# Gather of neighbours by one-hot tiles: a batch's sixteen tiles divided among GpSimd (4), VectorE (8) and ScalarE (4)

## The chip, the cores and the metric

The kernel runs on one core of one Trainium2 chip. The metric is the device time of one execution in microseconds (us); the lower the better. TensorE is called PE here, VectorE DVE, ScalarE ACT, GpSimd POOL, and SyncE SP, as in the profile.

## The reference

One layer of a network: a cross attention over a point cloud, then a state-space mixer, then a small feed-forward block. Only the first part matters here. It has 16 batches of 512 points with 32 features. Four space-filling curves (`M = 4` methods) give four orders of the points, and each point's neighbours are the 10 points of a window in each order:

```python
def _window_inds(sorted_idx, k=K):
    start = jnp.maximum(0, i - k // 2)
    end = jnp.minimum(N, i + k // 2 + 1)
    pos = jnp.minimum(start[:, None] + jnp.arange(k)[None, :], (end - 1)[:, None])
    return jnp.take(sorted_idx, pos, axis=1)
...
neigh = gather(feats, inds)
gf = jnp.concatenate([jnp.broadcast_to(center, (B, N, k, C)), neigh - center], axis=-1)
```

What is gathered goes into a small attention over each window, a linear map, a normalisation and a maximum. This is done for two layers, the second on the features that the first gives.

## The kernel before

The program runs in stages, with a barrier between each and the next: `keys_and_ranks` (the rank of each point in each order), then for each of the two layers `gather_windows` and `window_attention`, with `instance_norm` between the layers, then `join_features`, `mamba_prepare`, `mamba_mix` and `feed_forward`. The change touches `gather_windows` alone, which runs twice.

`gather_windows` puts the features of a batch into the order of each curve by matmul with one-hot matrices. For a batch there are 16 one-hot tiles, 4 methods by 4 tiles of 128 points: a tile is 128 points by `EXT` = 576 places (f16), with a one where the point's rank equals the place. There are two ways to make a tile:

- DVE compares `place` with the rank in one instruction (line 695).
- ACT takes the absolute value of the distance in one activation (`apart`, line 763, three buffers), then relu(1 - distance) in a second one (line 776).

Before the change DVE makes tiles 0 to 9 (`HOT = 10`) and ACT tiles 10 to 15 (`LATE = 6`). POOL only clears parts of `cen`, `cen16` and `QT` at the start (lines 665 to 669). ACT starts when these are cleared.

A batch passes through these steps. The order on each engine is that of its `step` function, which `steps` unrolls by four batches; `at(1)` is the batch before the one of `at(0)`.

- SP loads the batch's features `fb` (32 channels by 512 points), stores the centre copies `cen16`, and stores `QT` to DRAM in four transfers of 360 KB.
- PE turns `fb` so that points lie on partitions (`ptok`) and spreads it over the four methods (`pcen`). Then, for the batch before, it gathers: 64 matmuls of 288 columns with the one-hot tiles and the high and low halves `t16` and `l16` into `pext`, and raises `gathered`. It starts these when all tiles of that batch are there.
- ACT copies `t16`, makes its first two tiles, copies `pext` of the batch before into `ext` (line 795), makes the rest of its tiles and copies `pcen` into `cen` and `cen16` (lines 804, 805).
- DVE makes `l16` (line 688; for the first batch line 693, in the middle of its tiles), its tiles, and then for the batch before the subtraction of the centres from the windows: three of 1710 columns into `QT` (line 707) and a small one (line 712).

The tiles have two buffers, by the batch's parity. `gathered` begins at 2 and counts gathers: whoever writes tiles of batch b waits for `gathered >= b + 1`, the end of the gather of batch b - 2. `ext`, `cen` and `QT` have four buffers.

Other lines that the prediction speaks of: in the window attention POOL subtracts a maximum (`Dm`, line 1069) while DVE reduces (lines 1029, 1033). In the mixer DVE splits a weight (`Wo`, line 2025) and POOL adds squares (`sqsum`, lines 2078, 2082). In the feed-forward block DVE splits `u` (line 2285) while POOL adds to `uf` (line 2313).

Of the kernel before, what the change touches and what calls it, by code (L numbers as in the profile page):

```python
# [10 lines left out]
ALU = mybir.AluOpType  # L11
ACT = mybir.ActivationFunctionType
X = mybir.AxisListType.X

B, S, D = 16, 32, 512
N = D
C = S
NT = N // 128
M = 4
# [526 lines left out]
def steps(eng, step, T, U):  # L546


    for s in list(range(U)):
        step(s % U, lambda lag, s=s: (s - lag, (s - lag) // U) if 0 <= s - lag < T else None)  # L550
    with eng.Fori(1, T // U) as i:
        for k in range(U):
            step(k, lambda lag, k=k: (i * U + (k - lag), i + (k - lag) // U))
    for s in range(T, T + U):
        step(s % U, lambda lag, s=s: (s - lag, (s - lag) // U) if 0 <= s - lag < T else None)


def gather_windows(nc, io, scratch, layer, O, feats, runs, perm, rank, fixed):


    with ExitStack() as ctx:
        def sb(name, shape, dt=F32):
            return ctx.enter_context(nc.sbuf_tensor(name + layer, shape, dt))
# [3 lines left out]
        def sem(name):  # L567
            used.append(ctx.enter_context(nc.semaphore(name + "_gw" + layer)))
            return used[-1]

        H2 = EXT // 2
        ident, rep, place = (fixed[name] for name in ("ident", "rep", "place"))
# [3 lines left out]
        onehot = sb("onehot", [128, 2, M * NT, EXT], F16)  # L576
        apart = sb("apart", [128, 3, EXT], F16)
# [17 lines left out]
        rank_turned = sem("rank_turned")  # L595
        apart_ready = sem("apart_ready")
        late_hot = sem("late_hot")
        gathered = sem("gathered")
        ext_ready = sem("ext_ready")
        cen_ready = sem("cen_ready")  # L600
        q_v = sem("q_v")
        q_out = [sem(f"q_out{k}") for k in range(4)]
        QV = PTS + 1
        HOT = 10
        LATE = M * NT - HOT
        SL = 128 // O
        QO = 16 * (M + 2)
        ZEROS = 6
# [8 lines left out]
        def first(b):  # L617

            return isinstance(b, int) and b == 0

        def late(b):

            return isinstance(b, int) and b >= B - 2
# [38 lines left out]
        @block.gpsimd  # L662
        def _(pool):
            for tile in (cen, cen16):
                nc.gpsimd.memset(tile[:, :, LEAD:LEAD + 1], 0.0).then_inc(zeroed, 1)
                nc.gpsimd.memset(tile[:, :, N + 1:PADN], 0.0).then_inc(zeroed, 1)
            turns = QT[:, :, :, :].rearrange("p k g x -> p k (g x)").rearrange("p k (w x) -> p k w x", x=32 * RES)
            nc.gpsimd.memset(turns[:, :, :, PTS * K * RES:], 0.0).then_inc(zeroed, 1)
            nc.gpsimd.memset(turns[:, :, NSUB // RES:, 0:PTS * K * RES], 0.0).then_inc(zeroed, 1)
            pool.wait_ge(zeroed, ZEROS)  # L670
            for k in range(4):
                pool.sem_inc(q_out[k], QO)

        @block.vector
        def _(dve):
# [6 lines left out]
            def step(k, at):  # L682
                if at(0):
                    (b, _), h = at(0), k % 2
                    dve.wait_ge(gathered, b + 1)
                    if not first(b):
                        dve.wait_ge(t16_ready, b + 1)
                        v.tensor_tensor(l16[:, h, :], ptok[:, h, 0:NT * C], t16[:, h, :],
                                        ALU.subtract).then_inc(l16_ready, 1)
                    for mt in range(HOT):  # L690
                        if first(b) and mt == HOT // 2:
                            dve.wait_ge(t16_ready, b + 1)
# [25 lines left out]
        @block.tensor  # L718
        def _(pe):
            pe.sem_inc(f_used, 2)  # L720
            pe.sem_inc(gathered, 2)

            def step(k, at):
                if at(0):
                    (b, i), h = at(0), k % 2
                    pe.wait_ge(f_in[h], (i * 32 + 16 * (k // 2 + 1)) * len(runs))
                    pe.wait_ge(l16_ready, b + 1)
                    pe.wait_ge(cen_ready, b + 1)
                    for t in range(NT):
                        last = nc.tensor.matmul(ptok[:, h, t * C:(t + 1) * C], fb[:, h, t * 128:(t + 1) * 128],  # L730
                                                ident[:, :], start=True, stop=True)
                    last.then_inc(tokens_out, 1)
                    nc.tensor.matmul(pcen[:, h, 0:N], rep[:, :], fb[:, h, :], start=True, stop=True).then_inc(f_used, 1)
                if at(1):
                    (b, _), k = at(1), (k - 1) % 4
                    h = k % 2
                    pe.wait_ge(l16_ready, b + 3)
                    pe.wait_ge(hot_ready, b * HOT + HOT)
                    pe.wait_ge(late_hot, b * LATE + LATE)
                    pe.wait_ge(ext_ready, b + 1)  # L740
                    for e in range(2):
                        for n in range(2 * NT):
                            half, t = (t16, l16)[n // NT], n % NT
                            for m in range(M):
                                last = nc.tensor.matmul(pext[m * C:(m + 1) * C, h, e, 0:H2],
                                                        half[:, h, t * C:(t + 1) * C],
                                                        onehot[:, h, m * NT + t, e * H2:(e + 1) * H2],
                                                        start=n == 0, stop=n == 2 * NT - 1)
                    last.then_inc(gathered, 1)

            steps(pe, step, B, 4)

        @block.scalar
        def _(act):
            act.sem_inc(cen_ready, 2)
            act.sem_inc(ext_ready, 2)
            act.wait_ge(zeroed, ZEROS)
            act.wait_ge(rank_turned, 2)

            def distance(b, j):  # L760

                mt = HOT + j
                nc.scalar.activation(apart[:, j % 3, :], place[:, :], ACT.Abs,
                                     bias=minus_rank[:, bass.ds(b + perm[mt // NT] * B, 1), mt % NT])\
                    .then_inc(apart_ready, 1)

            def hots(b, h, j0, j1):

                if j0 == 0:
                    distance(b, 0)  # L770
                for j in range(j0, j1):
                    if j + 1 < LATE:
                        act.wait_ge(late_hot, b * LATE + max(j - 1, 0))
                        distance(b, j + 1)
                    act.wait_ge(apart_ready, b * LATE + (j + 1))
                    nc.scalar.activation(onehot[:, h, HOT + j, :], apart[:, j % 3, :], ACT.Relu, scale=-1.0,
                                         bias=unit[:, :]).then_inc(late_hot, 1)

            def step(k, at):
                if at(0):  # L780
                    (b, i), h = at(0), k % 2
                    if first(b):
                        act.wait_ge(gathered, b + 1)
                        hots(b, h, 0, 2)
                    act.wait_ge(tokens_out, b + 1)
                    act.wait_ge(gathered, b + 1)
                    nc.scalar.activation(t16[:, h, :], ptok[:, h, 0:NT * C], ACT.Copy).then_inc(t16_ready, 1)
                    if not first(b):
                        act.wait_ge(late_hot, b * LATE)
                        hots(b, h, 0, 2)  # L790
                if at(1):
                    (b, _), k1 = at(1), (k - 1) % 4
                    act.wait_ge(gathered, b + 3)
                    act.wait_ge(q_v, b * QV + QV)
                    nc.scalar.activation(ext[:, k1, :].rearrange("p (e x) -> p e x", e=2), pext[:, k1 % 2, :, 0:H2],  # L795
                                         ACT.Copy).then_inc(ext_ready, 1)
                if at(0):
                    (b, i), h = at(0), k % 2
                    hots(b, h, 2, LATE)
                    act.wait_ge(f_used, b + 3)  # L800
                    act.wait_ge(q_out[k], i * QO + QO)
                    act.wait_ge(q_v, b * QV + QV)
                    for s0, n0, n1 in RUNS:
                        nc.scalar.activation(cen16[:, k, s0:s0 + n1 - n0], pcen[:, h, n0:n1], ACT.Copy)
                        last = nc.scalar.activation(cen[:, k, s0:s0 + n1 - n0], pcen[:, h, n0:n1], ACT.Copy)
                    last.then_inc(cen_ready, 1)
                if at(3) and late(at(3)[0]):
                    (b, r), k3 = at(3), (k - 3) % 4
                    act.wait_ge(q_v, b * QV + 5 * QV)
                    for m in range(M // 2, M):  # L810
                        store_windows(act, k3, r, m)

            steps(act, step, B, 4)
# [1683 lines left out]
```

## Time and profile before

| | us |
|---|---|
| median of 3 runs | 2252.63 (2251.91 to 2253.1) |
| the profiled execution | 2251.6 |
| its span | 2249.8 |
| busy PE, DVE, ACT, POOL | 1857.1, 1865.7, 1620.7, 1007.2 |

The profile is of one execution; the span runs from its first to its last recorded instruction. A timeline row has its start, its duration, engine, line of the program, what it writes and reads with the shapes, how many instructions were merged into it (x5) and, in brackets, how long the engine had been idle and who ended the wait. A row that merges several instructions lasts from the first's start to the last's end.

### The profile page before, as it was taken

To read this page: it belongs to the slowest core of one execution; us is meant where nothing else is said; L and a number is where in the kernel's file an instruction comes from. 1 tells how busy PE (TensorE), PEld (TensorE's weight loads), DVE (VectorE), ACT (ScalarE), POOL (GpSimd) and SP (SyncE) were. 2 spreads that over 40 slices of the span, in tenths; PEclk is the share of its full clock that TensorE was granted. 3 is DMA by queue.
4 is the path that set the end of the run, shared out by engine and by line. 5 is a ranking of instruction groups with operands and counts; after the bars stand their busy time and mean duration, and the time that the engine had idled before them with its cause. 6 is when DMAs were issued, how large, how long until landed. Compare 5 with 4: busy or idle time off the path is not lost. (4 is left out here: it accounts for less than half of the span.)

```text
span 2249.8 us, 100270 instructions
## 1 busy us (share of the span) xinstructions
PE 1857.1 (83%) x37656; PEld 1296.1 (58%) x37656; DVE 1865.7 (83%) x3775; ACT 1620.7 (72%) x3324; POOL 1007.2 (45%) x995
## 2 busy tenths in 40 slices
PE   3866648888886665699999997687999999999957
PEld 1333347777775433599999996333544454454422
DVE  8879969999997798688888887865888888888874
ACT  5889948888886998699999996465455455555432
POOL 0000048999995000578888884002433444344412
PEclk9996679999998666899999998899999999999988
DMA  1127666555563477645555551203222222222210
GB/s 36 30 65 169 163 146 126 119 125 122 120 125 72 94 171 164 133 101 107 107 107 107 107 107 38 95 10 96 85 80 84 75 84 81 82 84 75 65 55 19
DMA packets 434892, 215.50 MB, mean 96 GB/s; under 512 B 301195, under 2 KB 404267, under 8 KB 434680
## 3 DMA queue, kind: packets, MB, share of 16 engines
q1 hardware_dynamic: 430272, 210.76, 39.8%
q10 hardware_dynamic: 4536, 3.66, 0.6%
q8 instruction: 48, 0.79, 0.2%
q14 instruction: 36, 0.29, 0.0%
HBM read 161.35 MB, written 52.86 MB: 95 GB/s over the span
## 5 line engine op out<-in xcount | busy, mean ns | idle before, releaser
L973 PE MATMUL pQ<-QM,QX 128*128 128x64 f16 (+1 forms) x5760 | 532.4, 217 | 1.6 <-issue 1.6
L971 PE MATMUL pQ<-neigh_lo,QX 128*128 128x32 f16 (+1 forms) x5760 | 520.9, 189 | 2.8 <-issue 2.8
L971 PEld LDWEIGHTS pQ<-neigh_lo,QX 128*128 128x128 f16 x5760 | 496.0, 103 | 5.2 <-issue 2.5
L973 PEld LDWEIGHTS pQ<-QM,QX 128*128 128x128 f16 x5760 | 487.8, 104 | 2.5 <-issue 2.3
L1069 POOL TENSOR_TENSOR Dm<-Sc,mx 128x450 f32<-128x450 f32 x384 | 365.9, 953 | 80.6 <-DVE mx L1029 80.6
L1076 POOL TENSOR_TENSOR Ap<-E,R 128x450 f32<-128x450 f32 x384 | 365.8, 953 | 68.0 <-DVE R L1042 57.8
L1106 ACT ACTIVATE Vs<-pQ 128x480 f32<-128x480 f32 (+1 forms) x384 | 295.7, 770 | 5.7 <-PE pH L999 4.1
L1038 DVE STREAM_TRANSPOSE AT<-Ap 128x480 f32<-128x480 f32 x384 | 259.2, 675 | 33.3 <-PE pH L999 10.9
L2067 POOL TENSOR_TENSOR MT<-cb,decay 128x512 f32 (+1 forms) x128 | 163.9, 1302 | 244.2 <-PEq L1835 147.4
L1119 ACT ACTIVATE E<-Dm 128x450 f32<-128x450 f32 x384 | 224.3, 584 | 60.5 <-POOL Dm L1069 60.4
L1029 DVE TENSOR_REDUCE mx<-Sc 128x15 f32<-128x450 f32 x384 | 223.8, 583 | 16.5 <-ACT Sc L1100 16.5
L1033 DVE TENSOR_REDUCE Z<-E 128x15 f32<-128x450 f32 x384 | 233.5, 608 | 0.0
L1100 ACT ACTIVATE Sc<-pQ 128x450 f32<-128x450 f32 x384 | 209.2, 545 | 14.7 <-PE pQ L973 14.6
L999 PE MATMUL pH<-AT,Vs 128*32 128x30 f32 x17280 | 177.2, 197 | 47.5 <-DVE AT L1038 41.9
L999 PEld LDWEIGHTS pH<-AT,Vs 128*32 128x32 f32 x17280 | 172.5, 110 | 67.8 <-DVE AT L1038 42.0
L707 DVE TENSOR_TENSOR QT<-ext,cen 128x1710 f16<-128x1710 f32 x96 | 180.6, 1936 | 28.5 <-ACT ext L795 23.9
L966 PE MATMUL pQ<-maskR,maskL 128*128 128x160 f16 (+1 forms) x960 | 143.1, 247 | 67.5 <-DMA QX<-scratch_q 40.5
L2082 POOL TENSOR_TENSOR sqsum<-sqsum,sq 128x512 f32<-128x512 f32 x56 | 85.0, 1518 | 245.4 <-ACT sq L1928 245.4
L1860 PE MATMUL pO<-Wo,yw 128*128 128x512 f16 x768 | 176.3, 379 | 13.9 <-DVE Wo L2025 13.9
L1842 PE MATMUL pG<-h,W 128*128 128x512 f16 x768 | 178.2, 382 | 9.3 <-DVE W L2049 8.4
L2035 DVE SCALAR_TENSOR_TENSOR cv_m<-pX,taps_m,cv_m 128x496 f32<-128x496 f32 (+2 forms) x192 | 137.6, 717 | 51.7 <-ACT cv_m L1937 33.5
L1942 ACT ACTIVATE hid<-cv_m 128x512 f32<-128x512 f32 x64 | 40.3, 630 | 189.5 <-DVE cv_m L2035 189.5
(382 smaller groups left out, 3743.3 us busy)
## 6 DMA issues: line engine op xcount, KB each, us to landing
QM<-scratch_q SPq DMA_DIRECT2D x192, 240.0 KB, 2.7
QX<-scratch_q SPq DMA_DIRECT2D x768, 60.0 KB, 2.4
scratch_q<-QT SPq DMA_DIRECT2D x120, 360.0 KB, 4.8
Wg<-in_in_proj SPq DMA_DIRECT2D x64, 256.0 KB, 2.7
Wh<-in_in_proj SPq DMA_DIRECT2D x64, 256.0 KB, 2.8
Wo<-in_out_proj SPq DMA_DIRECT2D x64, 256.0 KB, 2.7
W_s<-in_in_proj SPq DMA_DIRECT2D x16, 256.0 KB, 2.7
CT<-scratch_c SPq DMA_DIRECT2D x192, 11.2 KB, 2.2
```

The lines of the kernel that those rows point to most:

```text
L707: v.tensor_tensor(flat[:, 0:W3, n * K:(n + 1) * K, :], rows(ext, k, LEAD * K + HALF - 1 + n, (PTS * RES, W3), (1, K), (PTS, RES)), rows(ce ...
L971: nc.tensor.matmul(pQ[:, p, u // PB, o + 32:o + BW], qx[u], W["neigh_lo"][:, 0:O], start=False, stop=True, skip_group_check=True)
L973: last = nc.tensor.matmul(pQ[:, p, u // PB, o:o + BW], qx[u], qm[u], start=False, stop=True, skip_group_check=True)
L999: last = nc.tensor.matmul(pH[at0:at0 + 32, p, 32 * u:32 * u + PTS * K], Vs[:, first + slot, u * O + 32 * half:u * O + 32 * half + 32], AT[ ...
L1029: v.tensor_reduce(mx[:, p, :], valid(Sc[:, p, :]), X, ALU.max).then_inc(max_ready, 1)
L1033: v.tensor_reduce(Z[:, p, :], valid(E[:, p, :]), X, ALU.add).then_inc(summed, 1)
L1038: v.transpose(AT[:, k5 % NA, :], A[:, k5 % ND, :]).then_inc(turned, 1)
L1069: nc.gpsimd.tensor_tensor(valid(Dm[:, p, :]), valid(Sc[:, p, :]), mx[:, p, :].unsqueeze(2).to_broadcast([128, SUBS, PTS * K]), ALU.subtrac ...
L1076: nc.gpsimd.tensor_tensor(valid(A[:, p, :]), valid(E[:, p, :]), R[:, p, :].unsqueeze(2).to_broadcast([128, SUBS, PTS * K]), ALU.mult).then ...
L1100: nc.scalar.activation(like(Sc[:, (k - 1) % ND, :], 32, PTS * K), blocks(p, 0, PTS * K), ACT.Copy)\
L1106: nc.scalar.activation(like(Vs[:, kv % RV, :], O, O), blocks(p, 32, O), ACT.Copy).then_inc(vs_ready, 1)
L1119: nc.scalar.activation(valid(E[:, p, :]), valid(Dm[:, p, :]), ACT.Exp, scale=32.0 ** -0.5).then_inc(exped, 1)
```

## The change

POOL takes four tiles (`ASIDE = 4`), DVE keeps eight (`HOT = 8`), ACT keeps four (`LATE = 4`). The tiles in order are 0 to 7 by DVE, 8 to 11 by POOL, 12 to 15 by ACT. POOL's comparison is the same instruction as DVE's, with the same waits on `gathered`. Its loop over the batches is written out: 64 instructions per stage after the clearing. PE waits for POOL's tiles also, by a new semaphore.

```diff
+        aside_hot = sem("aside_hot")
...
-        HOT = 10
-        LATE = M * NT - HOT
+        HOT = 8
+        ASIDE = 4
+        LATE = M * NT - HOT - ASIDE
...
             for k in range(4):
                 pool.sem_inc(q_out[k], QO)
+            for b in range(B):
+                pool.wait_ge(gathered, b + 1)
+                for mt in range(HOT, HOT + ASIDE):
+                    at = b + perm[mt // NT] * B
+                    nc.gpsimd.tensor_scalar(onehot[:, b % 2, mt, :], place[:, :], rank[:, at, mt % NT:mt % NT + 1], None,
+                                            ALU.is_equal).then_inc(aside_hot, 1)
...
                     pe.wait_ge(late_hot, b * LATE + LATE)
+                    pe.wait_ge(aside_hot, b * ASIDE + ASIDE)
...
-                mt = HOT + j
+                mt = HOT + ASIDE + j
...
-                    nc.scalar.activation(onehot[:, h, HOT + j, :], apart[:, j % 3, :], ACT.Relu, scale=-1.0,
+                    nc.scalar.activation(onehot[:, h, HOT + ASIDE + j, :], apart[:, j % 3, :], ACT.Relu, scale=-1.0,
```

## Rows read from the trace of the kernel before

**Rows 1.** Groups by line and shape: busy us, mean ns, idle before.

```profile
L776 ACT ACTIVATE onehot<-apart,unit_g 128x576 f16<-128x576 f16 x192 | 165.7, 903 | 0.0
...
L695 DVE TENSOR_SCALAR onehot<-place,rank 128x576 f16<-128x576 f16 x320 | 96.1, 378 | 0.0
```

**Rows 2.** Timeline of DVE (start us, duration us), the two stages' ends.

```profile
126.39 3.42 DVE L695 TENSOR_SCALAR onehot<-place,rank 128x576 f16<-128x576 f16 x5
...
294.39 0.23 DVE L712 TENSOR_TENSOR QT<-ext,cen 128x60 f16<-128x60 f32 x1
...
734.14 3.42 DVE L695 TENSOR_SCALAR onehot<-place,rank 128x576 f16<-128x576 f16 x5
...
902.16 0.23 DVE L712 TENSOR_TENSOR QT<-ext,cen 128x60 f16<-128x60 f32 x1
```

**Rows 3.** Stretches: us; PE, PEld, DVE, ACT, POOL busy; PEclk, DMA, GB/s.

```profile
200.00:248.75 48.75, 32.19 (x371) 19.66 (x371) 44.45 (x76) 48.75 (x91) 0.00 (x0) 0.61 0.72 169
```

**Rows 4.** Timeline of ACT, two activations in a row.

```profile
210.48 0.91 ACT L763 ACTIVATE apart<-place,minus_rank 128x576 f16<-128x576 f16 x1
211.15 0.92 ACT L776 ACTIVATE onehot<-apart,unit_g 128x576 f16<-128x576 f16 x1
```

**Rows 5.** Timeline of DVE, one batch.

```profile
210.87 5.64 DVE L707 TENSOR_TENSOR QT<-ext,cen 128x1710 f16<-128x1710 f32 x3 [0.50 <-ACT ext L795]
...
216.85 0.29 DVE L688 TENSOR_TENSOR l<-ptok,t 128x128 f16<-128x128 f32 x1
217.06 2.88 DVE L695 TENSOR_SCALAR onehot<-place,rank 128x576 f16<-128x576 f16 x10
```

**Rows 6.** Timeline of PE from one gather to the next.

```profile
147.39 1.15 PE L745 MATMUL pext<-onehot,t 128*32 128x288 f16 x16 [2.01 <-ACT onehot L776]
...
151.35 1.91 PE L730 MATMUL ptok<-ident_g,fb 32*128 32x32 f32 x8
153.08 2.05 PE L733 MATMUL pcen<-fb,rep 32*128 32x512 f32 x2
157.14 1.15 PE L745 MATMUL pext<-onehot,t 128*32 128x288 f16 x16 [2.01 <-ACT onehot L776]
```

**Rows 7.** DVE lines (ns min/median/max), and timelines of POOL and DVE.

```profile
L2025 DVE SCALAR_TENSOR_TENSOR Wo<-Wo x64: 676/1755/1765, 1561.8 to 2158.3; 128x512 f16<-128x512 f32 x64
...
1804.08 1.44 POOL L2082 TENSOR_TENSOR sqsum<-sqsum,sq 128x512 f32<-128x512 f32 x1 [7.54 <-ACT sq L1928]
...
1804.31 1.76 DVE L2025 SCALAR_TENSOR_TENSOR Wo<-Wo 128x512 f16<-128x512 f32 x1
...
L2285 DVE TENSOR_TENSOR u_f<-u_f x9: 1195/1199/1203, 2197.5 to 2227.8; 115x512 f16<-115x512 f32 x9
L2285 DVE TENSOR_TENSOR u_f<-uf_f,u_f x3: 692/693/693, 2195.6 to 2220.1; 115x512 f16<-115x512 f32 x3
```

**Rows 8.** Timelines of ACT, DVE and PE, start of the first stage.

```profile
129.13 1.44 ACT L763 ACTIVATE apart<-place,minus_rank 128x576 f16<-128x576 f16 x2 [10.29 <-POOL QT L669]
...
132.97 1.48 DVE L695 TENSOR_SCALAR onehot<-place,rank 128x576 f16<-128x576 f16 x5
...
137.63 1.15 PE L745 MATMUL pext<-onehot,t 128*32 128x288 f16 x16 [1.99 <-ACT onehot L776]
...
142.56 1.94 DVE L707 TENSOR_TENSOR QT<-ext,cen 128x1710 f16<-128x1710 f32 x1 [0.76 <-issue]
```

**Rows 9.** A line of POOL (ns min/median/max).

```profile
L1069 POOL TENSOR_TENSOR Dm<-Sc,mx x384: 941/952/962, 311.2 to 1375.1; 128x450 f32<-128x450 f32 x192
```

**Rows 10.** Groups of POOL by line and shape.

```profile
L2078 POOL TENSOR_TENSOR sqsum<-sq,zero_m 128x512 f32<-128x512 f32 x8 | 8.4, 1045 | 31.8 <-ACT sq L1928 31.8
...
L2313 POOL TENSOR_TENSOR uf_f<-uf_f,u_f 115x512 f32<-115x512 f32 x9 | 11.4, 1266 | 57.5 <-DVE u_f L2280 57.5
...
L1058 POOL MEMSET QX<- 128x1920 f32 x4 | 6.7, 1700 | 0.0
...
L1056 POOL MEMSET QX<- 128x960 f32 x2 | 1.8, 902 | 0.0
```

## Prediction

> **What bounds the kernel now.** I read the list of costliest instruction groups first, because it says where the edited lines run and how much time they hold. The gather's lines are a small part of the program: the sixteen tiles of a batch are 320 comparisons on DVE and 192 pairs of activations on ACT [rows 1], over 16 batches in each of two gather stages. DVE's first and last instructions of the stages lie at 126.4 and 294.6 us and at 734.1 and 902.4 us [rows 2], so some 336 of the 2249.8 us can be touched.
>
> Second, the table of stretches, for five batches in the steady part of the first stage. ACT is busy 48.75 of 48.75 us, DVE 44.5, PE 32 at a granted clock of 0.61, POOL not at all, and the DMA engines 0.72 of the time [rows 3]. ACT sets the pace, but DVE is at 91%: it is the next limit, only 9% away.
>
> Third, the timeline of one batch, which turns shares into a period: PE begins a gather at 147.39 and the next at 157.14 us [rows 6], 9.75 us apart. An activation on 576 columns starts 0.67 us after the one before it, although each is recorded as lasting 0.9 us [rows 4]: durations on ACT overlap, so spacing is the price. Twelve of them are 12 x 0.665 = 8.0 us, and the remaining 1.75 us are ext, the centre copies and t16. DVE's batch is 5.98 us from the first subtraction into QT to the l16 subtraction, 0.21 us for that, 10 tiles spaced (2.88 - 0.37) / 9 = 0.279 us apart (0.37 being one alone), and the rest of the 9.75 us, 0.7, is waiting for ACT [rows 5]. PE's batch, where it doesn't wait, is 3.96 us of matmuls into pext (147.39 to 151.35) and 3.78 us for ptok and pcen (to 155.13), 7.7 us in all [rows 6].
>
> **ACT's part.** Two of six pairs go, so 4 x 0.665 = 2.66 us per batch: ACT's own need falls from 9.75 to 7.1 us.
>
> **DVE's part, alone.** Two of ten tiles go, 0.56 us: 5.98 + 0.21 + 8 x 0.279 = 8.42 us per batch. DVE would set the period even if POOL's tiles cost it nothing, since PE needs 7.7 us and ACT 7.1. DMA work per batch is 0.72 x 9.75 = 7.0 us, below all of these.
>
> **POOL's part.** It adds 64 comparisons per stage, read from place (SBUF) and written to onehot. POOL waits for nothing but `gathered`, so those of batch b start when the gather of b-2 has ended; DVE's tiles for b-1 lie ahead of the same point, and POOL has more than a period for four instructions. POOL issues no DMA here and nothing but the next tiles is queued behind its wait. PE's additional wait costs nothing, by that slack. So the cost isn't POOL's time. It is what POOL's instructions do to DVE's.
>
> The trace shows that. At 1804.3 us DVE's subtraction into Wo (both inputs in SBUF) takes 1.76 us while POOL's sum, begun at 1804.08, runs; its shortest is 0.68 and its median 1.76. POOL's sum takes 1.44 us there, 1.26 where it is alone, and at the end of the program the subtraction into u_f takes 1.20 us beside POOL's sum and 0.69 without it [rows 7, 10]. So two such instructions exclude each other, and back to back they take turns. The comparison into onehot shows it too: the first five of the stage take 3.42 us while POOL clears QT (ACT is released by the last clearing at 129.13), the next five 1.48 [rows 2, 8]. Against that, POOL's 384 subtractions Dm stay within 941 and 962 ns although DVE's reductions, with one SBUF input, fill that stage [rows 9]: those don't collide. The subtraction into QT (ext and cen, both in SBUF) is of the Wo kind, and the tiles are of the other colliding kind. That is 5.9 + 2.2 of DVE's 8.42 us. DVE will have no idle time in which POOL could slip in, so each of POOL's four instructions delays DVE once per batch.
>
> **The price of one collision.** Wo loses 1.76 - 0.68 = 1.08 us to a POOL instruction that takes 1.26 us when it is not held up [rows 7, 10]: the price c is POOL's duration p less 0.18 us. No row shows a comparison on POOL. From below: a clearing of 960 and 1920 f32 columns takes 902 and 1700 ns, 0.83 ns a column, so 576 columns that are only written would take 0.58 us; c = 0.40. From above: two full inputs, 512 columns in 1.26 us, so 576 in 1.42; c = 1.24. With one of its two inputs a repeated column it was 1045 ns for 512, so 1.17 for 576 [rows 10]. One input read and one output written lies between 0.58 and 1.17; I take p = 0.9, c = 0.72.
>
> The Trainium skill (GPSIMD Engine Reference, Elementwise — side-by-side cycle accounting) gives about 1.8 cycles of 1.2 GHz per element for a tight loop; an estimate from that page is 0.86 us for 576, which would make the total 2280. The trace has no row for it. The skill's page SBUF — State Buffer, section Who interferes with whom, says that the shared port pair is held for the full instruction and that the loser fully blocks. By that rule c would be all of 0.9 us and the total 2304; the Wo row has 0.18 us less, and I go by the row.
>
> **The start of a stage.** POOL's clearings end at 129.1 us as before [rows 8]. ACT then has 8 activations instead of 12 before the first gather, which started at 137.6 us [rows 8]: 2.7 us earlier at best. But POOL goes on to batch 1 at once, in the middle of DVE's second group of tiles for batch 0, and collides up to three times (2 us). I put the first subtraction into QT, which started at 142.56 us, at 140.5.
>
> **The sum.** From there to the end DVE does 14 times 8.42 us and the last two QT groups (5.98 + 5.91): 129.8 us; and 56 of the 64 collisions fall into it (batches 2 to 15): 56 x 0.72 = 40.3 us. The stage's last DVE instruction then ends at 140.5 + 129.8 + 40.3 = 310.6 us where it ended at 294.6 [rows 2]; the same arithmetic for before, 142.56 + 15 x 9.75 + 5.9, gives 294.7. So +16.0 us per stage. The second stage took as long, 168.2 us [rows 2], so +32 us. The period would be 8.42 + 2.88 = 11.3 us. The profiled execution took 2251.6 us, 1.0 below the median; 2251.6 + 32 = 2283.6, with that 1.0 some 2284 us. Bounds: c = 0.40 gives 292.7 us for the stage's end, -4 us in total, 2248; c = 1.24 gives 339.7, +90, 2342. The change breaks even at c = 0.43 (p = 0.61), close to the lower bound.
>
> **Rivals.**
> *No collisions.* POOL's single SBUF input doesn't get in the way of DVE. DVE's 8.42 us set the period; the first QT starts at 139.8; the end is 139.8 + 129.8 = 269.6, 25 us earlier per stage: 2202 us. For it: all POOL rows beside which a DVE instruction runs long have two inputs or none. Against it: the clearing has none and delayed the tiles.
> *Only the tiles collide, the QT subtractions don't.* This is the mechanism that ends on the other side at a middling price: the gather ends 3.9 us after the tiles, 2.1 us of QT work are left, and of POOL's 3.6 us about 1.5 reach into the tiles, two collisions, 1.4 us a batch. The period is 9.8 us, yet start and tail gain: 139.8 + 129.8 + 14 x 1.4 = 289.2, 5.4 us earlier per stage, 2241 us. It decides if QT stays at 1.94 us with a POOL instruction beside it. Against it: the rows of Wo and u_f, which are of QT's kind [rows 7].
> *POOL's comparison is slower than the two-input rows*, say 2 us for f16 and a comparison: c = 1.82, 56 x 1.82 = 102 us, 2406 us. Nothing in the trace speaks for it but the missing row.
>
> **How the numbers follow.** 0.76 for the forecast (own range 2248 to 2342), 0.09 for no collisions, 0.08 for tiles only, 0.07 for the slow comparison. A difference of 0.2% (4.5 us) is about what a measurement of this kernel can tell from no change. Of the forecast's 0.76 some 0.06 lie within that, near its lower bound, and 0.01 below. Faster is 0.09 + 0.08 + 0.01 = 0.18, same 0.06, slower 0.69 + 0.07 = 0.76. The range runs from just under the tiles-only case to the upper bound: 2238 to 2340.
>
> **What would show it.** In the changed profile: QT subtractions with POOL beside them at 1.94 + 0.7 = 2.6 us, some tiles at 1.1 us instead of 0.37; ACT waiting for `gathered` before ext; a period of 11.3 us; the stage's last subtraction at about 310 us; POOL comparisons near 0.9 us alone and longer by the DVE instruction they wait for. QT all at 1.94 us, or a period under 9.7, would prove me wrong; POOL comparisons at 0.6 us would leave the mechanism and take away the loss.

## The result, and the profile after

| | before | after |
|---|---|---|
| median, us | 2252.86 (2251.91 to 2253.12, 4 runs) | 2285.41 (2282.41 to 2289.04, 4 runs) |
| ratio, 95% interval | | 1.0135 (1.0117 to 1.0154) |
| span of the profiled execution, us | 2249.8 | 2283.5 |

The change makes the kernel 1.35% slower, 33 us, where 32 us were forecast. The first thing to see is the ends of the two stages. Timeline of DVE in the changed kernel, the rows that answer to [rows 2] and, for the first subtraction into QT, to [rows 8]:

```profile
141.64 1.94 DVE L715 TENSOR_TENSOR QT<-ext,cen 128x1710 f16<-128x1710 f32 x1 [0.66 <-issue]
...
311.75 0.23 DVE L720 TENSOR_TENSOR QT<-ext,cen 128x60 f16<-128x60 f32 x1
...
935.16 0.23 DVE L720 TENSOR_TENSOR QT<-ext,cen 128x60 f16<-128x60 f32 x1
```

The first stage ends at 311.98 us, 17.4 later than before (294.62). The second, whose first tile now starts at 750.26, takes 185.1 us where it took 168.2. So the whole loss lies in the two gather stages: 17.4 + 16.9 = 34.3 us, where the span grew by 33.7. The table of stretches for 200 to 290 us, before and after (columns as in [rows 3]):

```profile
200.00:290.00 90.00, 56.18 (x656) 34.26 (x656) 79.01 (x127) 85.37 (x158) 0.00 (x0) 0.59 0.72 167
```

```profile
200.00:290.00 90.00, 56.40 (x608) 36.54 (x612) 89.70 (x104) 59.02 (x115) 90.00 (x34) 0.58 0.60 141
```

ACT is relieved (59 us instead of 85). DVE is busy 89.7 of 90 us with fewer instructions, and POOL is busy all the time. TensorE's granted clock is nearly the same, 0.59 and 0.58. Whose instructions became longer stands in the list of groups, after (the tiles were 378 ns in [rows 1]):

```profile
L679 POOL TENSOR_SCALAR onehot<-place,rank 128x576 f16<-128x576 f16 x128 | 340.4, 2678 | 1.0 <-POOL QT L671 1.0
L715 DVE TENSOR_TENSOR QT<-ext,cen 128x1710 f16<-128x1710 f32 x96 | 193.1, 2063 | 1.2 <-issue 1.0
L703 DVE TENSOR_SCALAR onehot<-place,rank 128x576 f16<-128x576 f16 x256 | 148.0, 646 | 0.0
```

DVE makes 256 tiles instead of 320 and needs 148 us for them instead of 96. One batch shows how; DVE's timeline, one instruction a row, and POOL's under it:

```profile
284.18 0.28 DVE L696 TENSOR_TENSOR l<-ptok,t 128x128 f16<-128x128 f32 x1
284.38 0.35 DVE L703 TENSOR_SCALAR onehot<-place,rank 128x576 f16<-128x576 f16 x1
284.66 0.76 DVE L703 TENSOR_SCALAR onehot<-place,rank 128x576 f16<-128x576 f16 x1
285.34 0.84 DVE L703 TENSOR_SCALAR onehot<-place,rank 128x576 f16<-128x576 f16 x1
286.10 0.36 DVE L703 TENSOR_SCALAR onehot<-place,rank 128x576 f16<-128x576 f16 x1
...
288.12 0.78 DVE L703 TENSOR_SCALAR onehot<-place,rank 128x576 f16<-128x576 f16 x1
288.82 1.92 DVE L715 TENSOR_TENSOR QT<-ext,cen 128x1710 f16<-128x1710 f32 x1
290.67 2.40 DVE L715 TENSOR_TENSOR QT<-ext,cen 128x1710 f16<-128x1710 f32 x1
292.98 1.93 DVE L715 TENSOR_TENSOR QT<-ext,cen 128x1710 f16<-128x1710 f32 x1
294.95 0.57 DVE L720 TENSOR_TENSOR QT<-ext,cen 128x60 f16<-128x60 f32 x1
295.43 0.28 DVE L696 TENSOR_TENSOR l<-ptok,t 128x128 f16<-128x128 f32 x1
```

```profile
285.24 1.76 POOL L679 TENSOR_SCALAR onehot<-place,rank 128x576 f16<-128x576 f16 x1
286.98 1.76 POOL L679 TENSOR_SCALAR onehot<-place,rank 128x576 f16<-128x576 f16 x1
288.72 3.53 POOL L679 TENSOR_SCALAR onehot<-place,rank 128x576 f16<-128x576 f16 x1
292.23 4.27 POOL L679 TENSOR_SCALAR onehot<-place,rank 128x576 f16<-128x576 f16 x1
```

The period is 11.25 us (284.18 to 295.43); forecast was 11.3. But its parts are not those of the prediction. While POOL runs, two of three tiles of DVE start 0.68 to 0.76 us after the one before them instead of 0.28. Five such delays of 0.40 to 0.48 us, the last of them ahead of the first QT, stretch the eight tiles from 2.2 to 4.4 us. The three long subtractions into QT last 6.09 us in place of the 5.64 of [rows 5], by one of 2.40, and the small one 0.57 instead of 0.23 [rows 2]. That makes seven lengthened instructions of DVE in a batch, by 0.34 to 0.48 us each, for four tiles of POOL. POOL's tile lasts 1.76 us beside DVE's tiles and 3.5 to 4.3 us beside QT.

### The profile page after: what moved, and what is told of

The parts are those of the page before. It is cut to its first block and busy times, and to the rows that moved or that the text cites. A ratio compares the mean times of both kernels' runs of the same rounds, so it can differ in the third digit from the quotient of the medians.

```text
span 2283.5 us, 100046 instructions
## 1 busy us (share of the span) xinstructions
PE 1855.5 (81%) x37656; PEld 1302.3 (57%) x37656; DVE 1936.5 (85%) x3711; ACT 1538.6 (67%) x3196; POOL 1348.1 (59%) x1123
## 5 line engine op out<-in xcount | busy, mean ns | idle before, releaser
L679 POOL TENSOR_SCALAR onehot<-place,rank 128x576 f16<-128x576 f16 x128 | 340.4, 2678 | 1.0 <-POOL QT L671 1.0
L715 DVE TENSOR_TENSOR QT<-ext,cen 128x1710 f16<-128x1710 f32 x96 | 193.1, 2063 | 1.2 <-issue 1.0
L754 PE MATMUL pext<-onehot,t 128*32 128x288 f16 x1024 | 74.9, 442 | 133.4 <-POOL onehot L679 61.6
```

The source lines that it names most:

```text
L679: nc.gpsimd.tensor_scalar(onehot[:, b % 2, mt, :], place[:, :], rank[:, at, mt % NT:mt % NT + 1], None, ALU.is_equal).then_inc(aside_hot, 1)
```

## The experiments

The rival theory that this trace suggests is that POOL sets the pace itself: it never stands still, four of its tiles take a whole period, and PE's waits name it (8 waits, 30.5 us in the first stage, against 27.8 for DVE's tiles). I call the theory of the prediction A (DVE is lengthened, and DVE sets the time) and this one B.

### Four comparisons on POOL that nobody needs

```diff
 # the kernel before, 10 DVE, 6 ACT
+            for b in range(B):
+                pool.wait_ge(gathered, b + 1)
+                pool.wait_ge(spared, max(b * 4 - 4, 0))
+                for mt in range(8, 12):
+                    nc.gpsimd.tensor_scalar(spare[...], place[:, :], rank[...], None, ALU.is_equal).then_inc(spared, 1)
```

> The kernel before (tiles 10 DVE, 0 POOL, 6 ACT), and POOL makes four comparisons per batch into a spare buffer that nobody reads or waits for. Theory A (POOL's instructions lengthen DVE's, and DVE sets the time): DVE's own 8.98 us per batch plus the 2.83 us that the changed kernel's trace shows for four of POOL's tiles (11.25 - 8.42) is 11.8 us; the period goes from 9.75 to 11.8, 14 or 15 periods in two stages: +60 us, 2312 us. Theory B (POOL's own pace, 11.25 us for four tiles, holds back PE, and DVE's longer instructions are hidden): nobody waits for POOL here, so 2253 us, unchanged.

Measured: 2310.34 us, ratio 1.0243 (1.0217 to 1.0268). Nobody waits for POOL, PE's tiles all come from DVE and ACT, and still 57 us are lost. Nor is POOL at its own limit here: from the seventh batch on it stands idle for 3.5 to 3.8 us before each batch, waiting for the gather (75.2 us in 20 waits). B is refuted; A's 2312 was right. From DVE's timeline of this run, the tiles of one batch:

```profile
223.60 5.57 DVE L704 TENSOR_SCALAR onehot<-place,rank 128x576 f16<-128x576 f16 x10
```

Ten tiles last 5.57 us, where they last 2.88 in [rows 5]. The three subtractions into QT that follow last 5.63 us, as ever: in this run only 3 of the 48 of each stage are longer. The cost lands nearly whole on the tiles and on the small subtraction.

### Three tiles on POOL

```diff
-        ASIDE = 4
+        ASIDE = 3
```

> The changed kernel with POOL's fourth tile given to ACT (8 DVE, 3 POOL, 5 ACT). Theory A: DVE's 8.42 us plus 3 x 0.71 us = 10.55 us per batch; the stage's last DVE instruction at 141.6 + 14 x 10.55 + 11.9 = 301 us against 294.7 before: +13 us, 2266 us. Theory B: POOL's pace falls to 3 x 2.81 = 8.4 us, so the period is about 8.5 us and the total 2208 us, faster than before.

Measured: 2273.78 us, 1.0083 (1.0062 to 1.0104), far from B's 2208, and 8 us above A's 2266. DVE's timeline has the batch's small subtraction at these places:

```profile
224.45 0.65 DVE L720 TENSOR_TENSOR QT<-ext,cen 128x60 f16<-128x60 f32 x1
...
225.22 4.51 DVE L703 TENSOR_SCALAR onehot<-place,rank 128x576 f16<-128x576 f16 x8
...
235.31 0.65 DVE L720 TENSOR_TENSOR QT<-ext,cen 128x60 f16<-128x60 f32 x1
```

The period is 10.86 us, only 0.4 less than with four tiles: the eight tiles are still 4.5 us long, since two of the three POOL tiles fall beside them and the third reaches into them. Against the 8.24 us that DVE needs alone for eight tiles (shown below) that is 0.87 us for a POOL tile, not the 0.71 that I had carried over.

### POOL clears instead of comparing

```diff
 # against the run with four comparisons that nobody needs
-                    nc.gpsimd.tensor_scalar(spare[...], place[:, :], rank[...], None, ALU.is_equal).then_inc(spared, 1)
+                    nc.gpsimd.memset(spare[...], 0.0).then_inc(spared, 1)
```

> As the run with four spare comparisons, but POOL clears the spare buffer four times per batch (writes 576 columns, reads nothing). Theory A in the form of the prediction (any POOL instruction costs DVE its duration less 0.18 us): four clearings of about 0.6 us cost 1.7 us, period 10.7 us, +26 us, 2279 us. Theory A in a narrower form (a POOL instruction that only writes collides with DVE's tile comparisons but not with the subtraction into QT): the clearings start when a gather ends, which is when DVE does QT, and are over before its tiles: 2253 us. Theory B: 2253 us.

Measured: 2253.16 us, 0.9993 (0.9982 to 1.0003): nothing lost. POOL's line and DVE's line for QT in this run (ns min/median/max):

```profile
L679 POOL MEMSET spare<- x128: 573/573/1466, 129.3 to 877.7; 128x576 f16 x128
...
L714 DVE TENSOR_TENSOR QT<-ext,cen x96: 1932/1935/1942, 142.3 to 900.1; 128x1710 f16<-128x1710 f32 x96
```

Three of the four clearings of a batch run beside a QT subtraction, at 0.57 us, without either being longer. The first begins during DVE's last tiles and waits for them (1.08 to 1.47 us in the batches at 209.6, 218.8 and 228.8 us), and it costs them nothing. The prediction's price, the length of the POOL instruction less 0.18 us, is wrong for a clearing at these places.

### What POOL's comparison takes alone

```diff
 # the kernel before; ahead of POOL's clearings, 24 instructions, each waiting for the last
+            for n in range(24):
+                pool.wait_ge(widened, n)
+                form[n // 3]().then_inc(widened, 1)
```

> The kernel before, and at the start of each gather stage, ahead of POOL's clearings, 24 instructions on POOL alone, each waiting for the last, three of each form: clear 576 f32; comparison 576 f16 as in the change; multiplication instead of comparison; comparison of 288 columns; comparison f32 to f32; comparison with a constant instead of the rank; product of two f16 tiles; clear 576 f16. DVE stands still for most of it. What sets the 1.74 us of POOL's tile? If it is DVE's contention, the comparison takes the predicted 0.9 us here. If it is POOL's own speed, 1.72 us. If the comparison is slow and not the f16 or the column count, the multiplication takes about 0.9 to 1.2 us; if it is the f16, the f32 form does. The 288 columns take half, 0.9 us, if it goes by columns. The kernel is longer by the 24 instructions twice, some 50 to 60 us.

Measured once: 2316.68 us, 63 more than before (50 to 60 were expected). The groups of POOL in this run:

```profile
L670 POOL TENSOR_SCALAR spare<-place,rank 128x576 f16<-128x576 f16 x6 | 10.6, 1767 | 0.6
L671 POOL TENSOR_SCALAR spare<-place,rank 128x576 f16<-128x576 f16 x6 | 10.3, 1724 | 0.6
L673 POOL TENSOR_SCALAR wide<-wide,rank 128x576 f32<-128x576 f32 x6 | 10.3, 1721 | 0.6
L674 POOL TENSOR_SCALAR spare<-place 128x576 f16<-128x576 f16 x6 | 9.9, 1646 | 0.5
...
L675 POOL TENSOR_TENSOR spare<-place 128x576 f16<-128x576 f16 x6 | 6.9, 1148 | 0.5
...
L672 POOL TENSOR_SCALAR spare<-place,rank 128x288 f16<-128x288 f16 x6 | 6.0, 1002 | 0.6
...
L676 POOL MEMSET spare<- 128x576 f16 x6 | 3.5, 577 | 0.4
```

The comparison alone takes 1.72 us (line 670; its mean is 1767 ns because the first one of each stage ran beside DVE's tiles and took 1.86). It makes no difference whether it multiplies (line 671) or compares, or whether it reads f16 or f32 (line 673), and little whether the scalar is a constant (line 674, 1.65). Half the columns, 288, take 1.00 us, a little over half. The surprise is the order: this form with one full input is slower than the product of two (line 675; both inputs are the same tile), 1.15 us. The prediction had put it between the clearing, which reads nothing, and the sums of two inputs.

### One comparison beside the tiles, one beside QT

```diff
 # the kernel before; per batch two spare comparisons
+                for n, started in enumerate(((l16_ready, b + 3), (hot_ready, (b + 1) * HOT))):
+                    ...
+                    pool.wait_ge(*started)
+                    nc.gpsimd.tensor_scalar(spare[...], place[:, :], rank[...], None, ALU.is_equal).then_inc(spared, 1)
```

> The kernel before, and per batch two spare comparisons on POOL that nobody waits for: one released when DVE starts its tiles, one when DVE has finished them and starts the subtractions into QT. Theory A as predicted (each instruction waits for the other whole): both cost DVE the same, 1.56 us (1.74 - 0.18), and QT instructions reach 3.5 us. Theory A as the changed kernel's trace has it: the first costs DVE 0.9 us (two of its tiles at 0.76 to 0.84 us in place of 0.37), the second at most 0.5 us in one QT instruction or 0.3 us in the small one after them, and POOL's second comparison is the one that is stretched, to 3.5 us or more. ACT's pace leaves 0.7 to 0.9 us per batch free, so the total is 2255 to 2275 us.

Measured once: 2265.81 us, inside the 2255 to 2275 expected. POOL's timeline (first) and DVE's:

```profile
226.40 7.06 POOL L679 TENSOR_SCALAR spare<-place,rank 128x576 f16<-128x576 f16 x1 [1.72 <-DVE onehot L703]
233.45 1.76 POOL L679 TENSOR_SCALAR spare<-place,rank 128x576 f16<-128x576 f16 x1
```

```profile
226.16 1.93 DVE L715 TENSOR_TENSOR QT<-ext,cen 128x1710 f16<-128x1710 f32 x1
228.01 1.93 DVE L715 TENSOR_TENSOR QT<-ext,cen 128x1710 f16<-128x1710 f32 x1
229.86 1.93 DVE L715 TENSOR_TENSOR QT<-ext,cen 128x1710 f16<-128x1710 f32 x1
231.82 0.65 DVE L720 TENSOR_TENSOR QT<-ext,cen 128x60 f16<-128x60 f32 x1
232.39 0.28 DVE L696 TENSOR_TENSOR l<-ptok,t 128x128 f16<-128x128 f32 x1
232.59 0.35 DVE L703 TENSOR_SCALAR onehot<-place,rank 128x576 f16<-128x576 f16 x1
232.87 0.76 DVE L703 TENSOR_SCALAR onehot<-place,rank 128x576 f16<-128x576 f16 x1
...
236.68 1.93 DVE L715 TENSOR_TENSOR QT<-ext,cen 128x1710 f16<-128x1710 f32 x1
```

POOL's comparison begins 0.25 us after the first of the three QT subtractions and ends after the last, 7.06 us instead of 1.72, and none of the three is longer than 1.93. They don't take turns. But POOL's comparison is not cheaper there: DVE pays for it in the small subtraction (0.65 instead of 0.23) and in the second tile (0.76 instead of 0.37). So my expectation of "at most 0.5" for it was too low, and in this run the price is the same beside the tiles and beside QT, paid in two pieces of 0.4 us. The period was 10.52 us (the next batch's first QT starts at 236.68), against 8.80 for ten tiles with no POOL (9.08 less one tile, below): 0.86 us for each of the two.

### Four forms beside the tiles

```diff
 # the kernel before; one spare POOL instruction per batch, by turns
+                ...
+                pool.wait_ge(l16_ready, b + 3)
+                form(b, spare[:, b % 8, :])().then_inc(spared, 1)
```

> The kernel before, and one spare POOL instruction per batch, released when DVE starts its ten tiles (2.8 us), by turns: comparison of 576 columns, comparison of 288, product of two f16 tiles of 576 columns, clear 576. Alone these take 1.72, 1.00, 1.15 and 0.58 us. If an instruction on POOL keeps DVE out for its length less 0.18 us, as the prediction has it, ten tiles lengthen by 1.54, 0.82, 0.97 and 0.40 us, by turns. If only the parts of it in which it moves data do, the comparison of 576 costs 0.8 us and that of 288 half as much, 0.4; the product, which has no slow part, costs nearly its length, 0.9 to 1.0. If the cost is a fixed one per instruction, 288 columns cost 0.8 as well. Total within 0.2% of before, since ACT's pace leaves 0.9 us free.

Measured once: 2253.82 us, beside a kernel before of 2250.52 us: within the 0.2% expected. DVE's ten tiles beside, in order of time, the clearing, the comparison of 576 columns, that of 288 and the product (without POOL 2.88):

```profile
236.27 3.27 DVE L709 TENSOR_SCALAR onehot<-place,rank 128x576 f16<-128x576 f16 x10
...
246.30 3.71 DVE L709 TENSOR_SCALAR onehot<-place,rank 128x576 f16<-128x576 f16 x10
...
255.99 3.25 DVE L709 TENSOR_SCALAR onehot<-place,rank 128x576 f16<-128x576 f16 x10
...
265.53 3.78 DVE L709 TENSOR_SCALAR onehot<-place,rank 128x576 f16<-128x576 f16 x10
```

| POOL's instruction | alone, us | costs DVE, us |
|---|---|---|
| clear, 576 | 0.58 | 0.39 |
| compare, 576 | 1.72 | 0.83 |
| compare, 288 | 1.00 | 0.37 |
| product of two, 576 | 1.15 | 0.90 |

All groups of ten tiles of this run have these lengths by turns, to 0.02 us. The product and the clearing cost their length less 0.2 to 0.25 us, like Wo in [rows 7]; each lengthens one tile only. The comparison costs less than half its length, in two tiles: by 0.4 us each with 576 columns, by 0.17 and 0.22 us with 288.

### The same relief for ACT without POOL

```diff
-        HOT = 10      # 10 DVE, 6 ACT
+        HOT = 11      # 11 DVE, 5 ACT; in another run 12 and 4
```

> The kernel before with one tile given from ACT to DVE, none to POOL (11 DVE, 0 POOL, 5 ACT). ACT needs 10 x 0.665 + 1.75 = 8.4 us, DVE 5.98 + 0.21 + 11 x 0.279 = 9.26 us with nothing to collide with. Theory A (that is the sum with the collisions left out): period 9.26 us, the first gather 1.3 us earlier, 8 us less per stage, 2237 us. If instead the gather's time hangs on something else than the longer of the two engines (PE's clock, the stores), it stays near 2253 us.

> 12 tiles on DVE, none on POOL, 4 on ACT: the change with POOL's four tiles done by DVE. DVE alone sets the period: 9.08 + 0.28 = 9.36 us, ACT needs 7.1. 28 to 30 periods 0.28 us longer than with 11 on DVE, the first gather 1.3 us earlier twice: +6 us against that run, 2233 us. If DVE's four more comparisons cost what they did beside POOL (0.65 us each), 10.5 us and 2265 us.

Measured: 11 and 5, 2227.41 us, 0.9879 (0.9858 to 0.9901), where 2237 were expected; 12 and 4, 2237.30 us, 0.9917 (0.9896 to 0.9938), where 2233 were. Timelines of DVE, 11 first, then 12:

```profile
223.09 5.64 DVE L707 TENSOR_TENSOR QT<-ext,cen 128x1710 f16<-128x1710 f32 x3
...
228.90 0.28 DVE L688 TENSOR_TENSOR l<-ptok,t 128x128 f16<-128x128 f32 x1
229.10 3.15 DVE L695 TENSOR_SCALAR onehot<-place,rank 128x576 f16<-128x576 f16 x11
232.17 5.64 DVE L707 TENSOR_TENSOR QT<-ext,cen 128x1710 f16<-128x1710 f32 x3
```

```profile
225.03 5.64 DVE L707 TENSOR_TENSOR QT<-ext,cen 128x1710 f16<-128x1710 f32 x3
...
231.04 3.43 DVE L695 TENSOR_SCALAR onehot<-place,rank 128x576 f16<-128x576 f16 x12
234.39 1.94 DVE L707 TENSOR_TENSOR QT<-ext,cen 128x1710 f16<-128x1710 f32 x1
```

Periods of 9.08 and 9.36 us: a tile more on DVE costs 0.28, no more. The run with 11 beats both kernels, by 26 us and 58 us. It was better than the forecast 2237 for two reasons. The 5.98 us of [rows 5] from QT to l16 contained 0.17 us of waiting for ACT's t16 (here it is 5.81, 223.09 to 228.90). And I had left out the tail: before, DVE waited 3.79 us for the last ext (up to 288.71 us), and here it waits 0.1. Together that is some 6 us a stage, where 5 were missing. With 12 tiles ACT has the load that the change gives it and POOL's four tiles are on DVE: 2237 against 2285 us.

### One tile on POOL

```diff
-        HOT = 8
-        ASIDE = 4
+        HOT = 10
+        ASIDE = 1
```

> One tile on POOL, 10 on DVE, 5 on ACT, POOL starting at gathered as in the change. DVE alone would need 9.08 - 0.28 = 8.8 us, ACT 8.4. If a POOL tile costs DVE nothing or less than the 0.28 us that the tile costs on DVE itself, this beats the run with 11 on DVE and none on POOL (2227): about 2219 us. If it costs 0.9 us (beside DVE's tiles), the period is 9.7 us: 2247 us; if it falls beside QT, 0.3 to 0.5 us, the period is 9.1 to 9.3 us: 2228 to 2235 us.

Measured: 2241.14 us, 0.9952 (0.9935 to 0.9969), between the 2247 expected for a price of 0.9 us and the 2228 to 2235 for 0.3 to 0.5. The small subtraction, line 720, starts at 223.77 and 233.39 us in DVE's timeline, a period of 9.62 us, 0.82 more than the 8.80 of ten tiles without POOL:

```profile
223.77 0.65 DVE L720 TENSOR_TENSOR QT<-ext,cen 128x60 f16<-128x60 f32 x1
...
227.72 5.64 DVE L715 TENSOR_TENSOR QT<-ext,cen 128x1710 f16<-128x1710 f32 x3
233.39 0.65 DVE L720 TENSOR_TENSOR QT<-ext,cen 128x60 f16<-128x60 f32 x1
```

POOL's single tile started beside the third QT subtraction, ended after it, and cost what it costs beside tiles. A tile that DVE hands to POOL saves it 0.28 us and costs it 0.82. This division still beats the kernel before, by 13 us, because it too takes a tile from ACT; but giving that tile to DVE (2227) is 14 us better.

## Why the prediction was right

**The bound and ACT's part: right.** ACT was busy 59 of 90 us, 7.4 a period where 7.1 were forecast, and waited for the gather before ext (4.0 us at 281.98). DVE took over at once: from 141.64 us to the end of the first stage none of its instructions waits for another engine.

**DVE's own batch: 8.42 us forecast, 8.24 measured.** It is 9.08 less three tiles of 0.28. The step that was off is the 5.98 us, which held 0.17 us of waiting.

**What bounds after: right.** That the cost lies in what POOL does to DVE, and not in POOL's own time, is what the run with four unneeded comparisons shows (57 us lost with nobody waiting).

**POOL's slack: wrong.** The prediction gave POOL more than a period for its four tiles, started by `gathered`. In the changed kernel they fill the period: POOL is busy 90 of 90 us, and in half of the first stage's gathers POOL's tile is the last that PE waits for. That costs nothing only because DVE, which is just as full, waits for nothing there.

**The sum of the collisions: right by two errors that cancel.** Forecast were four of 0.72 us, 2.88; measured is 11.25 - 8.24 = 3.01, 0.75 each. The 0.72 came from p = 0.9 and c = p - 0.18. Both are wrong. p is 1.72 us, above even the upper bound of 1.42, because the prediction bounded an operation that no row showed by its number of inputs; with p = 1.72 its own rule would have given c = 1.54, a period of 14.6 us and 2376 us. And the rule, taken from a row of a two-input sum on POOL, doesn't hold for a comparison, which keeps DVE out for 0.83 us. That the total came out is luck: with the true length among the bounds, the range would have had to reach 2376. The prediction's rival of a slow comparison (2 us, 2406) had the length nearly right and the price wrong. The estimate that the prediction made from the Trainium skill (GPSIMD Engine Reference, Elementwise — side-by-side cycle accounting), 0.86 us, doesn't hold for this comparison; the measured length is twice that.

**Each waits for the other whole, in turns: wrong.** DVE's tiles wait for a part of POOL's comparison, twice 0.4 us. DVE's QT subtractions, back to back, hold POOL off (7.06 us) and hardly wait: in the changed kernel 28 of 96 are longer, by 0.47 us each. I had looked for QT at 2.6 us and tiles at 1.1; they are 1.93 to 2.40 and 0.76 to 0.84, five of eight. By the Trainium skill (SBUF — State Buffer, Who interferes with whom) whoever issues first holds the shared ports for the whole instruction and the other blocks. The runs agree for POOL behind one QT subtraction. They don't for the two QT subtractions that were issued after POOL's comparison and yet went ahead of it (7.06 us in place of 1.72), nor for DVE's tiles beside the comparison, 0.83 of 1.72 us. The same section says that an instruction that only writes doesn't collide with a two-input one; for the clearing beside QT (0.57 us, QT 1.935) the runs agree.

**The rival of tiles only, and the sign chosen to decide it.** The prediction said that QT at 1.94 us with a POOL instruction beside it would prove it wrong and give 2241 us. With three POOL tiles QT stays at 1.93 in all but two subtractions of a stage, in the run with one comparison beside each in all but one, and the loss is there all the same. What the rival had wrong is not QT but POOL: it took POOL's work beside QT to be free, and in these runs a comparison that begins there isn't finished until the short instructions come, which then pay for it.

**The start: 140.5 forecast, 141.64 measured.** The end was 310.6 forecast, 311.98 measured.

**Why four tiles cost 0.75 us each and one to three 0.82 to 0.87.** The lengthened instructions of DVE can be counted in the steady batches of the traces: two with one POOL tile, four with the two comparisons (10.52 us), six with three tiles, and seven with four, here and in the run where nobody needs them. So a POOL comparison lengthens two instructions of DVE, by 0.34 to 0.48 us each, but one of the four, the one whose second half lies beside a QT subtraction (288.72 to 292.25 us above), lengthens only one.

**Left open.** Why POOL's comparison keeps DVE out in two pieces of 0.4 us and not for its length isn't shown. With 288 columns both pieces are half as long, so they go with the columns. But the clearing and the product of two, with as many columns, lengthen one tile by most of their time (0.39 of 0.58 and 0.90 of 1.15 us), so length alone doesn't give the price, and no run separates reading from writing. Nor was it tried what lets one of three QT subtractions be longer with four tiles on POOL, when it isn't with one to three.

## What to carry to other kernels

Before an idle engine is given work, ask what it takes from the busy one: here DVE makes a tile itself in 0.28 us and loses 0.75 to 0.87 us when POOL makes it. With the same load on ACT, every division tried was slower with tiles on POOL than with them on DVE: 2241 (one) and 2274 us (three) against 2227, 2285 (four) against 2237. Moving one tile from ACT to DVE was worth more than any division with POOL that was tried. Measure an operation's length and its price to the neighbour separately, each for the very form: neither followed from the rows of other forms. And check a forecast that comes out right against its terms: this one hit the time with a length wrong by a factor of two. A sign that is meant to decide between two theories must be one on which they differ in time, and QT at 1.94 us wasn't.

## What the runs showed of the hardware that was not expected

- On POOL an operation with one tensor and one scalar is slower than a product of two tensors (here the same tile twice): 576 columns in 1.72 us against 1.15, the same for f16 and f32, for comparison and multiplication, and 1.65 with a constant for the scalar.
- A POOL comparison begun beside the first of DVE's three long two-input subtractions lasts 7.06 us, the subtractions 1.93 each as ever; it then costs DVE the same 0.8 us in the instructions after them.
- Clearing 576 columns on POOL costs DVE 0.39 us when begun with its tiles, and its two-input subtractions nothing.
